# Attention on one Trainium2 core: the value and ones products of a key tile, made one key tile later in TensorE's order

## What is computed

```
q = (x @ wq_w + wq_b).reshape(b, s, H, DH).transpose(0, 2, 1, 3)
k = jnp.einsum('bsl,hld->bhsd', k_lat, upk_w) + upk_b[None, :, None, :]
v = jnp.einsum('bsl,hld->bhsd', v_lat, upv_w) + upv_b[None, :, None, :]
scores = jnp.einsum('bhqd,bhkd->bhqk', q, k) / jnp.sqrt(jnp.float32(DH))
scores = jnp.where(causal[None, None], scores, -jnp.inf)
attn = jax.nn.softmax(scores, axis=-1)
out = jnp.einsum('bhqk,bhkd->bhqd', attn, v)
```

## Time and profile before

| what | us |
|---|---|
| median of the runs (3) | 2542.58 |
| lowest and highest | 2536.89, 2544.89 |
| the profiled execution | 2533.65 |
| its span on the core | 2532.1 |
| attention stage in it | about 301 to 1480 |
| one group of attention (units 16 to 19) | 143.7 |

### The profile page before, as it was taken

The page is one execution under the profiler, slowest core; times in us unless marked ns, Lnnn a source line. Parts: engine busy times, 40 slices in busy tenths (PEclk is TensorE's granted clock), DMA queues, the critical chain, the costliest instruction groups (busy, mean ns, idle before and its releaser), DMA issues. The chain is left out here.

```text
span 2532.1 us, 33323 instructions
## 1 busy us (share of the span) xinstructions
PE 2301.3 (91%) x11973; PEld 1450.3 (57%) x11973; DVE 1515.1 (60%) x3317; ACT 1042.6 (41%) x1925; POOL 1189.4 (47%) x765
## 2 busy tenths in 40 slices
PE   5998499999999999999999959999959999999997
PEld 5776244444444444444444336776747878788786
DVE  2665587677767677776767345555535555555553
ACT  2333045555555555555555632122113343333332
POOL 0000036566665656566565764344343544444543
PEclk8999599999999999999999979999979999999999
DMA  3766711313123131513121023343236656566561
GB/s 104 264 234 237 169 34 35 84 34 84 35 51 84 35 87 37 141 40 84 39 51 53 24 70 113 110 140 100 84 117 196 200 185 205 176 191 216 178 161 34
DMA packets 171610, 285.98 MB, mean 113 GB/s; under 512 B 30137, under 2 KB 72633, under 8 KB 171456
## 3 DMA queue, kind: packets, MB, share of 16 engines
q1 hardware_dynamic: 145152, 210.45, 28.5%
q0 software_dynamic: 26304, 73.54, 9.7%
HBM read 198.61 MB, written 92.38 MB: 115 GB/s over the span
## 5 line engine op out<-in xcount | busy, mean ns | idle before, releaser
L848 ACT ACTIVATE b_pt<-b_st 128x512 f32<-128x512 f32 (+3 forms) x1280 | 612.6, 535 | 485.5 <-DVE b_st L810 205.6
L665 POOL TENSOR_TENSOR b_acc<-b_acc,b_pt 128x1024 f32<-128x1024 f32 (+1 forms) x256 | 592.8, 2345 | 213.3 <-ACT b_pt L848 213.1
L789 DVE TENSOR_REDUCE b_mpart<-b_mx 128x1 f32<-128x512 f32 x768 | 512.3, 686 | 199.2 <-PE b_mx L905 196.7
L926 PE MATMUL b_st<-b_q,b_k 97*128 97x512 f32 (+2 forms) x1280 | 496.6, 401 | 74.8 <-ACT b_pt L848 54.6
L905 PE MATMUL b_mx<-b_k,b_q 96*128 96x512 f32 (+2 forms) x1280 | 508.1, 412 | 29.9 <-DVE b_mt L797 25.9
L905 PEld LDWEIGHTS b_mx<-b_k,b_q 96*128 96x128 f32 x1280 | 248.1, 195 | 284.4 <-DVE b_mpart L789 153.2
L926 PEld LDWEIGHTS b_st<-b_q,b_k 97*128 97x128 f32 x1280 | 241.8, 190 | 281.2 <-ACT b_pt L848 240.0
L939 PE MATMUL b_ob<-b_pt,b_v 128*32 128x512 f32 (+3 forms) x2560 | 302.2, 544 | 1.1 <-ACT b_pt L848 1.1
L786 DVE CUSTOM_DVE_ANT_0 b_unread<-b_mx,b_later 128x384 bf16<-128x384 f32 (+3 forms) x512 | 245.0, 485 | 89.2 <-PE b_mx L905 88.8
L665 POOL TENSOR_TENSOR b_acc<-b_pt 128x1024 f32<-128x1024 f32 x48 | 113.4, 2379 | 299.7 <-ACT b_pt L848 299.5
L69 PE MATMUL e_fb<-e_xh,e_w_guh 128*128 128x512 f32 (+1 forms) x552 | 220.4, 399 | 1.5 <-DVE e_xl L1744 1.5
(11 more groups left out here) (228 smaller groups left out, 3529.9 us busy)
## 6 DMA issues: line engine op xcount, KB each, us to landing
b_q<-scr_qh SPq DMA_DIRECT2D x64, 256.0 KB, 4.6
b_k<-scr_kh SPq DMA_DIRECT2D x64, 256.0 KB, 4.1
sw_gu<-in_L_ffn_w_gate_dram SPq DMA_DIRECT2D x12, 704.0 KB
sw_gu<-in_L_ffn_w_up_dram SPq DMA_DIRECT2D x12, 704.0 KB
a_xin<-in_L_attn_x_dram POOLq DMA_DIRECT2D x8, 1024.0 KB, 5.9
scr_qh<-a_qh SPq DMA_DIRECT2D x8, 1024.0 KB, 4.5
scr_ql<-a_ql SPq DMA_DIRECT2D x8, 1024.0 KB, 6.8
scr_kh<-a_kh SPq DMA_DIRECT2D x8, 1024.0 KB, 5.2
```

The lines of the kernel that those rows point to most:

```text
L665: g.tensor_tensor(out[:, :, lo:], so_far[:, :, lo:], pt[n % NPB][:, :, lo:], ALU.add).then_inc(s_add, 1)
L789: v.tensor_reduce(part, mxb[i % NMX][:, 0:w], AX.X, ALU.max).then_inc(s_red, 1)
L848: act.activation(pt[n % NPB][:, j, lo:], stb[:, (2 * n + j) % NST, lo:], ACT.Exp, scale=SCALE).then_inc(s_exp, 1)
L926: pe.matmul(stb[:, (2 * n + j) % NST, lo:], kb[:, h, at:at + P], qb[:, h, q * CH + lo:(q + 1) * CH], start=True, stop=True).then_inc(s_st, 1)
```

## The change

In PE's order `values(m)` stands at step 2m + 5 in place of 2m + 3, and `count_ones(m)` at step 2m + 6 in place of 2m + 4. All that follows from them moves along by two steps: `finish` and the read of the sums (`FINISH`), the read of the output on ACT, the stores on SP, and SP's loads of the next group's v. Scores, max items, masks, exponentials and POOL's list stay where they are. Behind the last step, PE has one key tile more left.

```
-FINISH = (2, 4, 4, 2)
+FINISH = (4, 6, 6, 4)
...
-                    at = n - 4
+                    at = n - 6
...
-                    done = unit_ending(n, 3)
+                    done = unit_ending(n, 5)
                     if done is not None:
                         store_out(done)
...
-                    done = unit_ending(n, 1)
+                    done = unit_ending(n, 3)
                     if done is not None:
                         read_out(done)
...
-                    if n % 2 == 0 and n >= 4:
-                        count_ones((n - 4) // 2)
-                    if n % 2 and n >= 3:
-                        values((n - 3) // 2)
+                    if n % 2 == 0 and n >= 6:
+                        count_ones((n - 6) // 2)
+                    if n % 2 and n >= 5:
+                        values((n - 5) // 2)
...
-                values(NS // 2 - 1)
-                count_ones(NS // 2 - 2)
-                count_ones(NS // 2 - 1)
+                for m in range(NS // 2 - 3, NS // 2):
+                    if m >= NS // 2 - 2:
+                        values(m)
+                    count_ones(m)
                 finish(NU - 1)
```

## The result

| | before | after |
|---|---|---|
| median of the runs | 2539.73 us (2535.55 to 2544.89, 4 runs) | 2565.52 us (2564.50 to 2569.19, 4 runs) |
| ratio, 95% interval | | 1.0115 (1.0098 to 1.0132), +29 us |
| profiled execution, its span | 2533.65, 2532.1 | 2569.19, 2567.6 |
| attention, first score to last `finish` | 1180.0 | 1210.7 |
| ahead of it; behind it | 300.8; 1051.3 | 303.2; 1053.8 |

So 30.6 of the 35.5 us between the two profiled executions arise in the attention stage.

A forecast was written before the change was run, and what follows sets the result against it. TensorE's work and its waits for exponentials were taken to bound the attention stage. Lost fill 53.6, less gained 28.1, plus VectorE 10.4 made +35.9 us on 2542.6: 2578 us, slower by 1.4%, range 2551 to 2604.

The forecast's parts named there:

- The bound: Attention stage: bound by TensorE's work and its waits, 51.3 us of them scores waiting for exponentials; moved products don't wait.
- The price of a fill and the places: Between a step's two scores: 1.09 us per full product; places losing fill cost 53.6 us, places gaining save 28.1.
- three places without reserve: q = 1 tile 5, q = 2 tile 4, q = 3 tile 4: each loses a full ones product, 1.09 us per group.
- q = 0, tile 2: Step with p = 0: ones product of 512 queries becomes 128 at a waiting place, losing 0.64 us per group.
- q = 3, tile 12: Step with p = 0: loses a full ones product with 0.64 us in reserve, a loss of 0.45 per group.
- VectorE: Max items, q = 2 and 3: TensorE comes earlier, meets the b_mx ring; half taken, 10.4 us, ends 0 and 21.
- Moved at no cost: `finish`, ACT's reads, SP's stores and v loads move without cost; TensorE's 4.0 us end wait hides the leftover value product.
- q = 1, tile 2: Place listed among those that gain fill: a gain of about 0.15 us per group.
- Repaid at the next wait: Rival, attention stage: later waits shrink; half repaid 2551 us, all repaid 2514; chances 0.10 part repaid, 0.07 all repaid.
- The waits don't depend on the fill: Rival, attention stage: it keeps the pace of ACT and VectorE, so no change, 2543 us; chance 0.08.
- The clock falls more often: Rival, narrow start of q = 0: more drops to 1.2 GHz add 12 to 36 us, 2590 to 2614; chance 0.15.
- The base: Whole kernel: the sum was set on the median of the runs, 2542.6 us, 8.9 above the profiled execution.

The follow-up runs named there:

- e4: Before, with TensorE taking the ones product of key tile 5 in place of 4 for q = 3, filling tile 8: 2528.98 us, ratio 0.9973.
- e10: Before, with key tile 3 in place of 2 for q = 3, emptying tile 4, the max items' plan held as before: 2545.64 us, ratio 1.0034.
- e5: Before, with only `finish` moved two steps later, for q = 0 to 2: 2538.05 us, ratio 0.9986.
- e2: Before, with only the value products, their reads, stores and v loads one key tile later: 2538.66 us, ratio 1.0017.
- e3: After, with ones tiles for q = 1 to 3 chosen anew so full products stand at the long waits again: 2525.70 us, ratio 0.9955 to before.
- e11: Before, with ones tiles changed to fill q = 3 tile 8 and q = 2 tile 9, the max items' plan held: 2517.11 us, ratio 0.9914.
- e1: Before, with only the ones products, `finish` and the reads of the sums one key tile later: 2579.65 us, ratio 1.0175.
- e6: Before, with ones tiles changed to fill q = 3 tile 8 and q = 2 tile 9, the plan moving along: 2531.82 us, ratio 0.9979.
- e7: e1 with one more ones product on TensorE (key tile 3, q = 1), taken from POOL: 2570.59 us, ratio 1.0135 to before.

## Why the prediction was right, and where it was off

**The bound.** "A longer lag buys them nothing" holds: the change gained only where more fill came to stand between two scores.

**The price of a fill and the places.** Right, place by place, as are the signs: the waits rose to 74.3 (about 75 forecast), and a group takes 147 to 151 us but for the first (148). +53.6 forecast and +50.4 measured, -28.1 and -27.1, with 1.09 per full product at each of the three places without reserve. `e4` and `e10` confirm that price for a single place from both sides (-8.2 and +8.5). One size was off: q = 0, tile 2, 5.1 against 2.0. There two of the eight groups had no wait before, so that they had something in reserve, and two fall into stretches at the lower clock, where the ones product that is left takes longer. At q = 3, tile 12 the reserve is 0.69 by its own rows (1037.23 less 1036.54), not 0.64, which makes 3.2; measured were 4.4.

**VectorE.** The one term that was wrong: 10.4 forecast, nothing measured, and about 5 gained at the max items. The step that failed is "I take half of it". Its lower end was right: VectorE followed, and the waits of max items that the prediction named as a sign didn't appear. I had counted the 0.26 of the earlier trace rows as its idle time, but in tiles 7 and 8 of q = 2 it idles 2.2 us in before (0.84, 0.76, 0.26 and 0.37), and in after, at full clock, 1.8. So it meets these items without a backlog, and no max item waits for it. I had looked only at how fast TensorE would come there, not at what VectorE does just ahead of it. The same isn't shown for the places of q = 3, where no wait of a max item came up either.

**Moved at no cost.** Right: `e5` lies within its error, `e2` has no wait for ACT's reads, and the 3.3 us of the last `finish` were 4.0. `e2` loses at q = 1, tile 2, where only the value product ahead of it has become a narrow one; in after the ones product moves too, and the place gains what was forecast.

**The rivals.** *Repaid at the next wait* falls: in `e10` and in after the losses arrive in full. *The waits don't depend on the fill* falls with `e3`, `e4`, `e10` and `e11`, which change little but the fill: against after or before, the waits fell by 34, 7 and 15 us in `e3`, `e4` and `e11` and rose by 7.5 in `e10`. These tables also change which exponentials POOL adds up, but TensorE's rows show the wait appear and vanish just where the product leaves and enters. The Trainium skill, "Perfetto Trace Analysis", section "Identifying Performance Opportunities", says that repeating bubbles can mean too few buffers; here 15 us of them went with the ring of 3 left as it was. Whether a larger ring would do the same wasn't run. *The clock falls more often* was given as another case of 12 to 36 us; it is part of this one. In the profiled execution of after it takes about 10 us more than in before, so that it fills the place of the VectorE term there: +35.9 forecast, +35.5 between the two, near by luck, for a reason that the sum didn't hold. In `e1` it is 24 us, half of what its stage loses. The Trainium skill, "TensorE: Matmul & The Clock Gate", section "A second HAM failure mode: psum-queue depth-cycling", tells of small idles between matmul groups that swing the clock, in a bf16 kernel; the stretches of 10.2 us in `e1` and `e6`, with no idle over 1.2 us in the ten microseconds ahead of them, agree with it. At the one long stretch that before and after share (q = 2, tile 1, near 1385 and 1418) there is an idle of 1.95 and 1.52 at the fall itself, a max item that waits for VectorE.

**The base.** I set the sum on the median of three runs, 2542.58. With a fourth it was 2539.73, which makes 3 of the 12 us between 2578 and 2565.52. The VectorE term makes the others: between the medians the change costs 25.8 us, close to the 25.5 of the fills alone (53.6 - 28.1). At an equal mean clock it is some 20 to 23, the fills less the 5 at the max items; the others go with the clock.

**What stays open.** What sets off a fall: its places repeat (the start of q = 0, the turn from q = 1 to q = 2, q = 2, tiles 1, 4, 7 and 9), but a few us of work more or less move them. And the mean clock differs between executions of one kernel; what moves it isn't shown.

## What to carry to other kernels

Where an engine feeds a chain of others and waits for it, moving independent work is worth what it does to the gap of each wait: list the waits, price the fill by start-to-start rows, and count both the places that lose and those that gain. Then turn it round, for the same list tells where the work should stand: here two entries of a table, with the plan of the other work held, were worth 22 us, of which 13 to 15 by the fill, on an engine that was 95% busy. Before testing such a table, look who else reads it, since a planner that evens out load will fill the gap that the test was to open. And if TensorE's clock isn't at 1.00 throughout, read the granted clock of each variant by stretch, or a gain of 17 us of waits can end as 5. Before you explain a difference between two profiled executions, see where each stands among the runs of its kernel: here the pair was 35.5 us apart and the medians 25.8.

## What was unexpected of the hardware

TensorE's clock fell to 1.2 GHz in stretches where the engine was 94% busy and had no idle time over 1.2 us ahead of it (`e1`, 664.70 to 684.70, clock 0.74). The low stretches last 3.4 us mostly, 6.8 or 10.2 at some places, in before too, and once 20.5 (`e3`, from 512.4). 8.7 us more work for TensorE made a kernel 9 us faster (`e7` against `e1`), since the low stretches shrank from 74.8 to 34.0 us. And executions of the same kernel differ by up to 17 us on one chip with the mean clock that they are granted, 0.953 to 0.962 in before.
